# Row statistics for a layer norm: by accumulated passes on ScalarE instead of the statistics instruction on VectorE

## The reference

```
out = _chunk_attn(q, k, v, masks, W_in, b_in, W_out, b_out) + x
mu  = mean(out, axis=2)
var = mean(square(out - mu), axis=2)
return (out - mu) * rsqrt(var + 1e-5)
```

```
idx = top_k(2 p.p - |p|^2 - |p|^2, 30)
...
agg = einsum('bnkc,bnk->bnc', xk, softmax(h))
return x + agg
```

## Time and profile before

| | |
|---|---|
| median of three runs | 5831.81 us |
| the profiled execution | 5827.65 us |
| its span, first to last instruction | 5825.8 us |
| VectorE (DVE) busy | 5315.0 us, 91% |
| TensorE (PE) busy | 4613.9 us, 79% |
| ScalarE (ACT) busy | 3901.7 us, 67% |
| GpSimd (POOL) busy | 2479.7 us, 43% |
| mean granted TensorE clock | 0.901 |

### The profile page before, as it was taken

How to read it: one execution, slowest core, us unless ns; L and a number is a source line. 1 busy time by engine, 2 the same in 40 slices (tenths; PEclk the granted TensorE clock), 3 DMA queues, 4 the chain that set the end, 5 groups by cost and what they waited for, 6 DMA issues and landing times. The chain is left out here.

```text
span 5825.8 us, 167066 instructions
## 1 busy us (share of the span) xinstructions
PE 4613.9 (79%) x62610; PEld 2686.8 (46%) x63182; DVE 5315.0 (91%) x7589; ACT 3901.7 (67%) x9258; POOL 2479.7 (43%) x3044
## 2 busy tenths in 40 slices
PE   6888888888888888888888888830185799999999
PEld 2444444444444444444444444420032666666666
DVE  7999999999999999999999999947898988888887
ACT  3777777777777777777777777753434666766766
POOL 3566666666667666666666666630000000000000
PEclk7999999999999999999999999965598899999999
DMA  0010001000100001000100010000000000000000
GB/s 30 16 31 17 16 17 31 16 17 17 31 17 16 17 20 27 17 16 17 31 16 17 17 31 16 9 5 0 0 0 0 30 26 30 26 32 30 26 30 26
DMA packets 135652, 114.61 MB, mean 20 GB/s; under 512 B 105328, under 2 KB 105840, under 8 KB 134640
## 3 DMA queue, kind: packets, MB, share of 16 engines
q1 hardware_dynamic: 134768, 102.73, 6.0%
HBM read 69.16 MB, written 33.55 MB: 18 GB/s over the span
## 5 line engine op out<-in xcount | busy, mean ns | idle before, releaser
L559 ACT ACTIVATE ohT<-oh_ps 128x512 bf16<-128x512 f32 x1920 | 1149.4, 614 | 439.9 <-PE oh_ps L453 314.2
L802 DVE MAX8 vals<-pd_sb 128x8 f32<-128x1024 f32 x1024 | 1203.7, 1214 | 138.5 <-ACT pd_sb L559 121.5
L807 DVE FIND_INDEX8 idx<-vals,pd_sb 128x8 uint16<-128x1024 f32 x1024 | 1245.1, 1219 | 0.0
L474 PEld LDWEIGHTS g_ps<-tparts,ohT 128*128 128x128 bf16 x23040 | 847.5, 97 | 343.8 <-issue 81.3
L809 DVE MATCH_REPLACE8 pd_sb<-vals,pd_sb 128x1024 f32<-128x1024 f32 x768 | 928.7, 1209 | 0.0
L474 PE MATMUL g_ps<-tparts,ohT 128*128 128x24 bf16 x23040 | 866.8, 174 | 68.3 <-issue 31.2
L1881 PEld LDWEIGHTS e_a_ps<-planes,e_oh 120*128 120x128 bf16 x24576 | 687.9, 97 | 292.8 <-issue 212.2
L1652 ACT COPY e_at<-e_a_ps 128x512 f32<-128x512 f32 x512 | 542.5, 1059 | 350.5 <-PE e_a_ps L1881 344.6
L1881 PE MATMUL e_a_ps<-planes,e_oh 120*128 120x32 bf16 x24576 | 702.5, 178 | 75.9 <-DVE e_oh L1809 46.8
L378 PE MATMUL pd_ps<-ctx_s 128*128 128x512 f32 x1024 | 639.2, 709 | 68.3 <-ACT pd_sb L559 65.8
L453 PE MATMUL oh_ps<-bitsT,code 128*128 128x512 bf16 x1348 | 549.8, 412 | 162.8 <-ACT bitsT L716 120.8
(11 more groups left out here) (234 smaller groups left out, 6654.0 us busy)
## 6 DMA issues: line engine op xcount, KB each, us to landing
ctx_s<-in_ctx SPq DMA_DIRECT2D x32, 512.0 KB, 4.6
maskb<-in_mask_Bx1x_ff SPq DMA_DIRECT2D x32, 512.0 KB, 6.3
x_s<-in_x SPq DMA_DIRECT2D x32, 512.0 KB, 5.5
y_spill<-y_s SPq DMA_DIRECT2D x32, 512.0 KB, 3.0
e_y<-y_spill SPq DMA_DIRECT2D x32, 512.0 KB, 3.9
out<-e_o SPq DMA_DIRECT2D x64, 256.0 KB, 2.0
table<-in_ctx SPq DMA_DIRECT2D x96, 4.0 KB, 5.9
pd_sb<-in_shape_constants SPq DMA_DIRECT2D x1, 1024.0 KB, 5.2
```

The costliest lines, as they stand in the source:

```text
L474: m = nc.tensor.matmul(found_ps[gi % 2][:, k % GK, t, :], ohT[:, k % OHR, bass.ts(t, P)], tparts[:, par, part, :], start=(part == 0), stop ...
L559: return nc.scalar.activation(dst, src, func, scale=scale, bias=bias)
L802: nc.vector.max(vals[:, i, :], pd_sb[:, (t + i) % RING, :]).then_inc(topk_step, 1)
L807: found = nc.vector.max_index(idx16[:, par, t + i, 8 * r:8 * r + 8], vals[:, i, :], work)
```

## The change

The statistics of a half of y are no longer taken by VectorE. ScalarE makes two passes over the half, each with an accumulated output: `Identity`, for the sum, and `Square` with minus the mean of half 0 as bias, for the sum of squared distances from that mean. For half 0 a small activation makes minus its mean between the two. What the passes write goes into the half of `x_s` that has been added and is not needed any more, so the load of the next x has to wait for them. The five sums of each row and batch stay in `row_acc`; joining the halves and taking the variance is done once for all batches at the start of `stage_e`, by six operations on VectorE. `row_stats`, `mv` and GpSimd's copy are gone.

```
-        stats_all = held("stats_all", [P, B, 2])
+        row_acc = held("row_acc", [P, 5, B])
...
                 if not first:
                     gate(sp, y_ready, b * 2, sp_gates)
-                sp.dma_start(x_s[:], x[b]).then_inc(x_landed, 16)
                 if not last:
                     load_mask(b + 1, 1 - par)
                 if not (isinstance(b, int) and b < 2):
                     gate(sp, g_done, (b - 1) * NG, sp_gates)
                 load_table(b, par)
+                if not first:
+                    gate(sp, row_summed, b * 2, sp_gates)
+                sp.dma_start(x_s[:], x[b]).then_inc(x_landed, 16)
...
                     if quarter == 2 and ongoing:
                         queries_keys(mv_, nb, nh)
+                    if t == 3 and not first:
+                        row_sums(b - 1, 1)
+                    if t == 6:
+                        row_sums(b, 0)
                     if t == 3 and not last:
                         squares(mv_, b + 1, 1 - par)
...
+            def row_sums(b, h):
+
+                gate(act, y_ready, b * 2 + h + 1, act_gates)
+                half, spent = y_s[:, h, :], x_s[:, bass.ts(h, HALF)]
+                one = bass.ds(b, 1)
+                nc.scalar.activation(spent, half, ACT.Identity, accum_out=row_acc[:, h, one]).then_inc(sum_step, 1)
+                if h == 0:
+                    gate(act, sum_step, b * 3 + 1, act_gates)
+                    move(row_acc[:, 4, one], row_acc[:, 0, one], scale=-1.0 / HALF).then_inc(sum_step, 1)
+                gate(act, sum_step, b * 3 + 2 + h, act_gates)
+                nc.scalar.activation(spent, half, ACT.Square, bias=row_acc[:, 4, one],
+                                     accum_out=row_acc[:, 2 + h, one]).then_inc(row_summed, 1)
...
             rows(tail, B - 1, 1)
+            row_sums(B - 1, 1)
...
-            def row_stats(b, h):
-                dve.wait_ge(y_ready, b * 2 + h + 1)
-                nc.vector.bn_stats(bnst[:, h, :], y_s[:, h, :]).then_inc(bn_step, 1)
-                if h == 1:
-                    if not (isinstance(b, int) and b == 0):
-                        dve.wait_ge(mv_kept, b)
-                    gate(dve, bn_step, b * 2 + 2, dve_gates)
-                    nc.vector.bn_aggr(mv[:], bnst[:].rearrange("p h s -> p (h s)")).then_inc(mv_ready, 1)
...
                         if t == 2 and r == 2 and not first:
                             digits(b - 1, 1 - par, 1)
-                            row_stats(b - 1, 1)
                         if t == 6 and r == 2:
                             digits(b, par, 0)
-                            row_stats(b, 0)
...
             act.wait_ge(ln_step, 1)
-            a.activation(rstd[:], stats_all[:, :, 1], ACT.Sqrt, bias=epsc[:]).then_inc(sd_ready, 1)
+            act.wait_ge(var_step, 6)
+            a.activation(rstd[:], row_acc[:, 3, :], ACT.Sqrt, bias=epsc[:]).then_inc(sd_ready, 1)
...
             v.memset(epsc[:], EPS).then_inc(ln_step, 1)
+            v.tensor_tensor(row_acc[:, 0, :], row_acc[:, 0, :], row_acc[:, 1, :], ALU.add).then_inc(var_step, 1)
+            v.tensor_tensor(row_acc[:, 2, :], row_acc[:, 2, :], row_acc[:, 3, :], ALU.add).then_inc(var_step, 1)
+            dve.wait_ge(var_step, 2)
+            v.scalar_tensor_tensor(row_acc[:, 4, :], row_acc[:, 0, :], 1.0 / T, row_acc[:, 4, :], ALU.mult, ALU.add).then_inc(var_step, 1)
...
-            v.scalar_tensor_tensor(nmr[:], stats_all[:, :, 0], -1.0, rstd[:], ALU.mult, ALU.mult).then_inc(ln_step, 1)
+            v.scalar_tensor_tensor(nmr[:], row_acc[:, 0, :], -1.0 / T, rstd[:], ALU.mult, ALU.mult).then_inc(ln_step, 1)
```

More of the change, by code:

```diff
@@ L133, in build, with stage_a @@
         idx_all = held("idx_all", [P, N], U16)
-        stats_all = held("stats_all", [P, B, 2])
+        row_acc = held("row_acc", [P, 5, B])
         last_bn = held("last_bn", [P, 2])
-        stage_a(nc, x, ctx, mask, w_in, b_in, w_out, b_out, consts, y_dram, cst, con, planes, idx_all, stats_all)
+        stage_a(nc, x, ctx, mask, w_in, b_in, w_out, b_out, consts, y_dram, cst, con, planes, idx_all, row_acc)
         stage_b(nc, con, planes, last_bn, w1, g1, b1, w2, g2, b2, w3, g3, b3)
-        stage_e(nc, con, planes, idx_all, stats_all, last_bn, y_dram, out)
-def stage_a(nc, x, ctx, mask, w_in, b_in, w_out, b_out, consts, y_dram, cst, con, planes, idx_all, stats_all):
+        stage_e(nc, con, planes, idx_all, row_acc, last_bn, y_dram, out)
+def stage_a(nc, x, ctx, mask, w_in, b_in, w_out, b_out, consts, y_dram, cst, con, planes, idx_all, row_acc):
     OHR = 3
@@ L193, in stage_a @@
         y_s = sb("y_s", [P, 2, HALF])
-        bnst = sb("bnst", [P, 2, 6])
-        mv = sb("mv", [P, 2])
         pd_ps = st.enter_context(nc.psum_tensor("pd_ps", [P, HALF], F32))
@@ L216, in stage_a @@
         dve_gates = sem("dve_gates")
+        act_gates = sem("act_gates")
         sp_gates = sem("sp_gates")
@@ L234, in stage_a @@
         y_ready = sem("y_ready")
-        bn_step = sem("bn_step")
-        mv_ready = sem("mv_ready")
-        mv_kept = sem("mv_kept")
+        sum_step = sem("sum_step")
+        row_summed = sem("row_summed")
         bits_ready = sem("bits_ready")
@@ L834, in _ @@
             digits(B - 1, 1, 1)
-            row_stats(B - 1, 1)
         @block.gpsimd
@@ L951, in emit @@
                         squares_split(b + 1, 1 - par, misc_base(b) + (12 if first else 16))
-                    if t == 5 and not first:
-                        gate(pool, mv_ready, b, pool_gates)
-                        nc.gpsimd.tensor_copy(stats_all[:, bass.ds(b - 1, 1), :].rearrange("p b s -> p (b s)"),
-                                              mv[:]).then_inc(mv_kept, 1)
             def normalise(s, t):
@@ L1018, in _ @@
             gather(B - 1, 1, 1, range(GROUPS), steps)
-            pool.wait_ge(mv_ready, B)
-            nc.gpsimd.tensor_copy(stats_all[:, B - 1, :], mv[:]).then_inc(mv_kept, 1)
             pool.wait_ge(g_done, B * NG)
-            pool.wait_ge(mv_kept, B)
 def stage_b(nc, con, planes, last_bn, w1, g1, b1, w2, g2, b2, w3, g3, b3):
@@ L1482, in _, with stage_e @@
                 dve.wait_ge(bn_ready, 3)
-def stage_e(nc, con, planes, idx_all, stats_all, last_bn, y_dram, out):
+def stage_e(nc, con, planes, idx_all, row_acc, last_bn, y_dram, out):
     NB = 16
@@ L1530, in stage_e @@
         ln_step = sem("e_ln_step")
+        var_step = sem("e_var_step")
         sd_ready = sem("e_sd_ready")
@@ L1687, in _ @@
             v.memset(epsc[:], EPS).then_inc(ln_step, 1)
+            v.tensor_tensor(row_acc[:, 0, :], row_acc[:, 0, :], row_acc[:, 1, :], ALU.add).then_inc(var_step, 1)
+            v.tensor_tensor(row_acc[:, 2, :], row_acc[:, 2, :], row_acc[:, 3, :], ALU.add).then_inc(var_step, 1)
+            dve.wait_ge(var_step, 2)
+            v.scalar_tensor_tensor(row_acc[:, 4, :], row_acc[:, 0, :], 1.0 / T, row_acc[:, 4, :], ALU.mult, ALU.add).then_inc(var_step, 1)
+            dve.wait_ge(var_step, 3)
+            v.tensor_tensor(row_acc[:, 4, :], row_acc[:, 4, :], row_acc[:, 4, :], ALU.mult).then_inc(var_step, 1)
+            dve.wait_ge(var_step, 4)
+            v.scalar_tensor_tensor(row_acc[:, 3, :], row_acc[:, 2, :], 1.0 / T, row_acc[:, 4, :], ALU.mult, ALU.subtract).then_inc(var_step, 1)
+            dve.wait_ge(var_step, 5)
+            v.tensor_scalar(row_acc[:, 3, :], row_acc[:, 3, :], 0.0, None, ALU.max).then_inc(var_step, 1)
             v.tensor_copy(iotan[:], con["iota"].rearrange("p (l o) -> p l o", o=1).to_broadcast([P, LO, 2])).then_inc(ln_step, 1)
```

## The result

The changed kernel takes 5871.36 us (median of six runs, 5851.01 to 5877.77) against 5830.22 us of the kernel before (six runs, 5822.1 to 5836.28): 1.0066 times as long, interval 1.0054 to 1.0077. It is slower by 41 us; 5878 was forecast. The profiled execution took 5867.16 us (span 5865.3), 39.5 us more than the profiled one before.

A forecast was written before the change was run, and what follows sets the result against it. The prediction took a ring of hand-overs between VectorE and ScalarE, not VectorE's busy time alone, to bound the kernel. Its terms, 39.9 - 0.6 + 0.5 + 1.0 + 1.1 + 6 = 48 us, gave 5878 us, range 5840 to 5925.

The forecast's parts named there:

- The ring: First stage: each batch is four stretches between tiles 3 and 7 and their maxima, each set by particular engines.
- Stretches 2 and 4: First stage, tile 7 to its maxima and tile 3 to its maxima: claimed to be set by VectorE.
- The 1.04 us of half 1: VectorE's half 1 statistics with the aggregate, behind tile 3's maxima: removal only lengthens the tile 7 wait, worth nothing.
- stretch 1: First stage, maxima of tile 3 to tile 7: claimed set by ScalarE and TensorE in all 30 middle batches.
- The rival by which VectorE's own time decides: First stage: VectorE's removed 1.65 us a batch come back 31 times, 51 us, giving 5779; chance 0.06.
- The sums: ScalarE's added passes in the first stage: claimed 1.60 us for half 1 and 1.92 us for half 0.
- Slot 3: Sums of half 1, between the last one-hot copy and the squares' copies: +0.95 us each batch, at tile 7.
- Slot 6: Sums of half 0, between keys and one-hot copies, before tile 7's exponentials: +1.37 us in batches where ScalarE sets it.
- stretch 3: Maxima of tile 7 to next tile 3: ScalarE's in one batch, VectorE's with 2.1 us to spare in the other.
- The ends: First batch -0.6 us, last batch +0.5, first stage's tail +1.0, six VectorE operations in the last stage +1.1.
- the last rival: Square outside ScalarE's loaded set: two table loads for each of 64 sums, 164 us, about 6040; chance 0.02.
- The clock: TensorE's granted clock in the first stage: new idle time was taken to cost 0.2 us a batch, 6 us.

The follow-up runs named there:

- e1: The kernel before without any row statistics, the last stage reading values set once: 5821.18 us, 0.9992 of the kernel before.
- e2: The changed kernel with VectorE's statistics put back beside ScalarE's sums, their result unused: 5844.67 us, 1.0037 of the kernel before.
- e3: The changed kernel without ScalarE's sums of half 1: 5829.63 us, 1.0001 of the kernel before.
- e6: The changed kernel with VectorE taking the maxima of odd tiles one search round earlier: 5827.92 us, 1.0002 of the kernel before.
- e12: The changed kernel with thirty small unused products on TensorE ahead of the scores of tile 4: 5807.77 us, 0.9962 of the kernel before.
- e7: The changed kernel with the sums of half 1 moved ahead of the exponentials of tile 3: 5799.19 us, 0.9944 of the kernel before.
- e5: The kernel before with VectorE taking the maxima of odd tiles one search round earlier: 5841.25 us, 1.0021 of the kernel before.
- e9: The kernel before plus ScalarE's two unused passes over half 1 ahead of tile 3's exponentials, x's load waiting for them: 5794.0 us, 0.9948.
- e11: The kernel before with thirty small unused products on TensorE ahead of the scores of tile 4: 5755.92 us, 0.9879 of the kernel before.

## Why the prediction came out right

**The ring** holds. ScalarE is tied to VectorE only by the maxima of tile 3 and tile 7, VectorE to ScalarE by the copies of tile 3 and tile 7, and each stretch has one engine that sets it. Stretches 2 and 4 are VectorE's: 21.38 and 21.37 us in both kernels.

**The 1.04 us of half 1 are worth nothing**: e1 takes them away and gets nothing, e2 puts them back and pays nothing in stretch 1. The rival by which VectorE's own time decides (5779) is out by e1 alone, and at the same low time e1 and the kernel before agree in that stretch to 0.03 us, one batch apart.

**The sums** were built from rows of other shapes at 1.60 and 1.92 us and measured 1.67 and 2.05. The passes fit (0.62 us for `Identity`, 0.72 for `Square`), the wait of the engine for itself was too small: 0.24 us where I had taken VectorE's 0.13; in half 0 there are two, 0.20 and 0.21.

**Slot 3**: predicted +0.95 us. Where the lower level stays away, the squares start 0.91 us later after the search of tile 3 (31.41 against 30.50). At tile 7 it is 0.85 us in the mean over 30 batches (stretch 1: 38.33 to 39.18), and at the same clock 0.64 to 0.87 (over all batches with 3.4 us of low time 0.73, with 13.7 us 0.75). "Nothing there takes up a delay" was a little too strict: in the batch at the good clock about 0.3 us are taken up in small pauses behind the turned bits.

**Slot 6** is the term that was most over-sized: predicted +1.37 us where ScalarE sets stretch 3. Measured 59.34 to 60.37 us from tile 7 to the next tile 3, +1.02, and part of that is the clock, whose low time there grew from 8.0 to 11.2 us. In the batches with 10.2 us of it the difference is 0.77 us (59.66 in five, 60.43 in four). So stretch 3 takes up more of a delay than the 0.55 us that I had counted; in which waits stays open. In the other batches VectorE gains its 0.60 us where it still has no wait (56.68 to 56.08), but 3 of 15 got a wait, so that the mean gain is 0.39. "Just enough" held in twelve; the three with a wait are ones whose stretch 3 had the most time at the lower clock. The waits named as signs were 4.6 us at tile 7 (measured 4.39 in the mean) and 3.2 us at tile 3 in every second batch (3.0 over 15, two of them without a wait). For two batches 2 x 0.85 + 1.02 - 0.39 = 2.33 us against 2.66.

**The ends** were small and are small, off by a us or two each; the start has the wrong sign (+1.3 for -0.6). The tail is +1.3 us for 1.0, the six operations +1.2 for 1.1; the other 1.9 us of the last stage lie within what that stage varies between kernels that do the same there (1301.0 to 1316.7 us for the last). The table load that the last rival feared did not come: `Square` runs beside exponentials and copies with no load between them (1045.77 in the timeline above). The Trainium skill, "ScalarE: Activation LUTs", section "Table sets: the hidden batching unit", says that functions of one set share a load, and no row of its table of sets names `Square` (a row on precision further down in that section does, beside identity and relu); this trace shows no load for it beside the functions in use.

**The clock** is the term that failed: +6 us predicted, and the low time of a batch is nearly the same, 15.02 and 15.48 us. That is two changes that cancel, and it was luck that the small term fitted them. The new waits that I feared do go with the lower level in stretch 3: from tile 7 to the next tile 3, in the 15 batches where ScalarE sets it, the low time is 11.2 us after and 8.0 before. It is 10.5 to 11.4 in after, e2, e3, e6 and e12, which have the sums of half 0 in slot 6, and 9.1 in e7, which has them too; without them it is 6.6 to 8.7 in seven kernels and 9.6 in e5. From tile 3 to tile 7 it went the other way, from 9.6 to 8.3 us, although TensorE stands longer behind the squares; why is open. The place whose edit changed the clock most is one that I had not named, the pause ahead of the scores of tile 4, and the change as made leaves that one nearly alone (1.75 and 1.87 us in the mean). Shortening it to 1.1 and 1.3 us in the mean went with 37 and 45 us less in the 30 middle batches (e9, e11), as much as the whole effect of the change.

**What this leaves.** The change costs 41 us as it stands; about 35 of them in the 30 middle batches, by ScalarE's longer chain and by more low time in stretch 3. e2 shows that some 20 us between two such kernels can go with the clock alone, so the terms read at the same low time (0.73 us for slot 3, 0.77 for slot 6) are better evidence than the close fit of the total, to which the cancelled clock helped. The same change with half 1 in slot 2 (e7) is the version that beats both kernels and computes all of it, 0.9944; the kernel before with the pause filled on TensorE (e11) is the fastest, 0.9879.

## What to carry to other kernels

Ask of each stretch between two hand-overs which engine's work ends last there, and count removed work only in the stretches that its engine sets: 53 us off the busiest engine were worth nothing that could be measured here, and the sums put on the second one (87 us of busy time) cost 41. Work that has to be added to an engine goes where that engine already stands waiting for the other; the same 1.67 us cost 0.9 us in slot 3 and 0.07 in slot 2. An edit of the order also changes what runs beside what: in e5 the same three instructions took 0.87 us longer. And look at which pause of TensorE an edit opens or closes, since that can outweigh the edit itself; before two kernels are compared by a few us in a stretch, compare stretches with the same time at the lower clock.

## What was not expected of the hardware

Work added can make a kernel faster: two unused passes on ScalarE gave 0.9948 (e9), thirty unused products on TensorE 0.9879 (e11). An activation that needs the accumulated result of the one before it stands for 0.20 to 0.24 us, and the accumulated read of a 512-element pass takes 0.19 us. An index instruction of VectorE (`hi`, 128x120) took 1.14 us in place of 0.29 when it came to run beside an instruction of GpSimd (e5); that this is the cause was not tested. The last stage lost 24 us of 1303 with its own code unchanged, when only the first stage had been edited (e11), and took 1282.9 us in e12; this is open.
